# Edge stages in 26 groups of pairs (23 of four, then three, two, one) in place of 25 (24 of four, one of two)

## What is computed

```
h = relu(layernorm(x)); x = x + relu(segment_sum(att * (cat(h[src], h[dst], e) @ Wm.T + bm), dst))   # layer 0, att: softmax over dst
h = relu(layernorm(x)); x = x + rst(h)       # layer 1: (segment_sum((h @ fc.T + b) * out_deg**-.5 [src], dst)) * in_deg**-.5 + h
h = relu(layernorm(x)); x = x + gcn2(h) + h  # layer 2: two GCN convolutions with self loops, relu between
h = relu(layernorm(x)); x = x + relu(gcn2(h) + h)  # layer 3: the same with other weights
```

## Time and profile before

| | us |
|---|---|
| time, median of 3 runs (2416.01, 2422.07, 2416.51) | 2416.51 |
| the profiled execution | 2418.93 |
| its span in the profile | 2417.1 |
| PE busy | 1823.6 (75%) |
| DVE busy | 1857.2 (77%) |
| ACT busy | 1381.3 (57%) |
| POOL busy | 1778.8 (74%) |

### The profile page before, as it was taken

One profiled execution on the slowest core, in us unless ns is written; L12 is line 12 of the kernel. 1 busy time (PEld: TensorE's weight loads), 2 busy tenths in 40 slices (PEclk: granted clock), 3 DMA queues, 4 the chain that ended last, 5 costly groups with the idle time before them and its releaser, 6 DMA issues.

```text
span 2417.1 us, 26454 instructions
## 1 busy us (share of the span) xinstructions
PE 1823.6 (75%) x6414; PEld 890.1 (37%) x6414; DVE 1857.2 (77%) x3047; ACT 1381.3 (57%) x3108; POOL 1778.8 (74%) x1776
## 2 busy tenths in 40 slices
PE   3888888874998378778999767768999788879700
PEld 1433443322444134334444333334444344434300
DVE  7999976646888577887999678877999699978500
ACT  2766776532887144436888534436888555548500
POOL 7777777776777777747777677747777577777777
PEclk9999999986999699889999888879999799989955
DMA  3344322225777345434444356554444354542200
GB/s 72 91 123 129 107 72 72 72 77 133 225 244 225 94 157 160 130 108 114 126 124 130 104 168 179 167 165 109 131 130 127 110 139 135 139 118 82 70 21 22
DMA packets 220666, 295.96 MB, mean 122 GB/s; under 512 B 78636, under 2 KB 84905, under 8 KB 220388
## 3 DMA queue, kind: packets, MB, share of 16 engines
q1 hardware_dynamic: 164068, 243.35, 30.9%
q0 software_dynamic: 56448, 50.92, 11.6%
HBM read 152.99 MB, written 141.77 MB: 122 GB/s over the span
## 4 chain that ended last, share of the span: by engine, by line
POOL 34%; issue 16%; DVE 15%; PE 5%; ACT 5%; DMA 1%; DVEq 0%; POOLq 0%; SPq 0%; ACTq 0%
POOL mn_ring L540 25%; POOL out_dram L1921 8%; PE bank L1210 4%; DVE node_h L1420 3%; DVE mn_total L1599 3%; DVE node_x L1444 1%; DVE mn_scaled L1615 1%; DVE node_h L1465 1%; ACT node_square L1339 1%; DVE mn_ring L1584 1%; DVE node_mean L1427 1%; ACT node_std L1323 1%; DMA mn_ring<-slot_rows,addr_i 1%; PE bank L1204 1%; DVE node_res L1438 1%
## 5 line engine op out<-in xcount | busy, mean ns | idle before, releaser
L540 POOL DMA_INDIRECT mn_ring<-slot_rows,addr_i x980 | 971.2, 991 | 375.3 <-issue 296.8
L1210 PE MATMUL bank<-node_x,center 128*128 128x512 f32 x492 | 254.4, 632 | 75.4 <-DVE node_h L1420 71.1
L1219 PE MATMUL bank<-node_h,wconv 128*128 128x512 f32 x492 | 272.1, 637 | 0.0
L1214 PE MATMUL bank<-node_square,mean 128*128 128x512 f32 x492 | 268.7, 629 | 3.7 <-ACT node_std L1318 2.8
L1339 ACT ACTIVATE node_square<-bank 128x512 f32<-128x512 f32 x246 | 145.6, 592 | 209.7 <-PE bank L1210 209.6
L540 POOL DMA_INDIRECT found<-node_table,look_i x196 | 209.4, 1068 | 72.5 <-issue 63.9
L1921 POOL DMA_INDIRECT out_dram<-keep,scat_i x196 | 200.0, 1020 | 62.4 <-issue 62.1
L540 POOL DMA_INDIRECT xin<-in_x_dram,src_i x192 | 194.9, 1015 | 63.1 <-issue 57.6
L1224 PE MATMUL bank<-node_act,wconv 128*128 128x512 f32 x442 | 239.0, 624 | 2.7 <-ACT node_act L1333 2.7
L540 POOL DMA_INDIRECT xin<-in_x_dram,dst_i x192 | 193.0, 1005 | 58.5 <-issue 58.5
L1333 ACT ACTIVATE node_act<-bank,bias 128x512 f32<-128x512 f32 x246 | 170.5, 693 | 93.1 <-PE bank L1219 92.9
(11 more groups left out here) (345 smaller groups left out, 3896.2 us busy)
## 6 DMA issues: line engine op xcount, KB each, us to landing
out_dram<-node_rows SPq DMA_DIRECT2D x98, 256.0 KB, 3.3
mn_rin<-res SPq DMA_DIRECT2D x96, 256.0 KB, 3.8
slot_rows<-node_rows SPq DMA_DIRECT2D x96, 256.0 KB, 2.1
slot_rows<-keep SPq DMA_DIRECT2D x96, 256.0 KB, 2.0
mn_fcol<-f_rows SPq DMA_DIRECT2D x192, 128.0 KB
node_x_in<-in_x_dram SPq DMA_DIRECT2D x76, 256.0 KB
res<-mn_x SPq DMA_DIRECT2D x72, 256.0 KB, 2.9
mn_ring<-slot_rows,addr_i POOLq DMA_INDIRECT x980
```

The lines of the kernel that those rows point to most:

```text
L540: return eng.indirect_dma_start(out=dest, out_offset=None, in_=table, in_offset=bass.IndirectOffsetOnAxis(ap=index, axis=0))
L1210: pe.matmul(bank[i][:, :], C["center"][:, :], src, start=True, stop=True).then_inc(s["centered"][i], 1)
L1214: pe.matmul(bank[4][:, :], C["mean"][:, :], nd.square[:, i - 1, :], start=True, stop=True) \
L1219: pe.matmul(bank[5 if i == 2 else 1][:, :], C["wconv"][:, 2 * i - 4, :], nd.h[i][:, u % 2, :], start=True, stop=True) \
```

## The change

A table `PAIRS` gives the number of pairs of each group: 23 groups of four, then three, two and one; `STEPS` = 26. `before(g)` is the number of pairs in front of group g. All of `main_phase` reads its sizes and offsets from these; so do `node_ticks`, `ORDER` and the last entry of `CLEAR`. The front phase and `LOCALS` stay with GROUPS = 25. With the new count of steps `node_ticks` gives the totals 23, 36, 61, 75, 100 after A to E and 117 before the last step of F, which takes 13. Steps 0 to 22 have a tick in A, C and E; in B the odd steps up to 21, in D the even steps up to 22; in F the last one before the lump is step 21 in place of 20. `AHEAD` grows from 22 to 24 units.

```diff
+PAIRS = [GP] * (HQ // GP - 1) + [3, 2, 1]
+STEPS = len(PAIRS)
...
-CLEAR = (16, 19, 21, 23, GROUPS - 1)
+CLEAR = (16, 19, 21, 23, STEPS - 1)
...
-        if g == GROUPS - 1:
+        if g == STEPS - 1:
             due += GAP[st]
-        elif g < GROUPS - QUIET[st]:
+        elif g < STEPS - QUIET[st]:
             due += SHARE[st]
-        upto = TICKS if (st, g) == ("F", GROUPS - 1) else min(int(due), TICKS)
+        upto = TICKS if (st, g) == ("F", STEPS - 1) else min(int(due), TICKS)
...
-ORDER = [(st, g) for st in STAGES for g in range(GROUPS)]
+ORDER = [(st, g) for st in STAGES for g in range(STEPS)]
...
+def before(g):
+
+    return sum(PAIRS[:g])
...
         def w_of(g):
-            return pairs_of(g) * P
+            return PAIRS[g] * P
...
         def of_group(a, g):
-            return a[:, g * W:g * W + w_of(g)]
+            return a[:, before(g) * P:before(g) * P + w_of(g)]
...
-        n = GROUPS
+        n = STEPS
...
-                                         0.0 if g == 0 else total[:, 1 - i % 2, W - 1:W], ALU.mult, ALU.add) \
+                                         0.0 if g == 0 else total[:, 1 - i % 2, w_of(g - 1) - 1:w_of(g - 1)], ALU.mult, ALU.add) \
...
                     for j in range(tiles(g)):
-                        t = 2 * GP * g + j
+                        t = 2 * before(g) + j
...
-                        q = upto * GP + pairs_of(upto) - 1
+                        q = before(upto + 1) - 1
```

More of the change, by code:

```diff
@@ L1505, in w_of @@
         def w_of(g):
-            return pairs_of(g) * P
+            return PAIRS[g] * P
         def tiles(g):
-            return 2 * pairs_of(g)
+            return 2 * PAIRS[g]
         def rows3(a, g):
@@ L1523, in scale @@
         def scale(col, g):
-            return wide(col, g, 2 * GP * g)
+            return wide(col, g, 2 * before(g))
         def flat(a):
             return a.rearrange("p (t f) -> (p t) f", f=F)
-        n = GROUPS
+        n = STEPS
         order, ticks = ORDER, TICKS_OF
@@ L1902, in fetch @@
                         gp.wait_ge(s["h_kept"][1], 16 * h_uses(n, 1))
-                    elif st == "B" and 2 * GP * (g + 1) > TILES - LOOK_LAST >= 2 * GP * g:
+                    elif st == "B" and 2 * before(g + 1) > TILES - LOOK_LAST >= 2 * before(g):
                         gp.wait_ge(s["late"], mark["all"])
@@ L1955, in turn_rows @@
                         pe.wait_ge(s["mixed"], i - n)
-                    for j in range(pairs_of(g)):
+                    for j in range(PAIRS[g]):
                         c = slice(j * P, j * P + P)
```

## The result

The changed kernel takes 2430.24 us (median of 6 runs, 2427.46 to 2434.50), against 2416.52 for the kernel before in the same comparison. The ratio is 1.0052, with a 95% interval of 1.0041 to 1.0064: 12.6 us slower, between 9.9 and 15.5 (the medians lie 13.7 apart). The forecast was 2433, or +16.4, and slower.

A forecast was written before the change was run, and what follows sets the result against it. The prediction took six runs of POOL plus four handovers, where compute drains, to bound the kernel. Its terms, 6.1 + 5.3 + 2.7 + 3.0 + 0.9 - 2.2 + 0.6 = +16.4 on the median 2416.51, gave 2433 us, range 2421 to 2442.

The forecast's parts named there:

- C to D: Handover from stage C to D: a tick in step 22, then smaller steps, 22.7 us for 16.6; +6.1 us (4.5 to 7.5).
- E to F: Handover from stage E to F: same shape as C to D, 24.3 us for 19.0; +5.3 us (4 to 7.5).
- B to C: Handover from stage B to C: four small finishes in place of three, 33.1 us for 30.44; +2.7 us (1.5 to 4.5).
- D to E: Handover from stage D to E: ticks move to even steps, scan 22 comes 3.4 us earlier; +3.0 us (0.5 to 7).
- sends: POOL's sends after F's gathers: five ticks leave this stretch at 0.55 us each; -2.2 us (-5 to 0).
- front and A: A to B handover +0.9 us (0 to 3.5); front phase, two more units, +0.6 us (0 to 1.5).
- the cover of 4.5 us: Before B's first gather: addresses ready 4.5 us ahead of it; they come 5.0 later, 0.5 over the cover.
- Only the last group counts: Rival: drains begin when the last gathers land, so a last group of one pair shortens them; -11 us, 2405; chance 0.07.
- The tick is mostly absorbed: Rival: slack behind POOL hides the tick in step 22; C and E pay 2 us each, D nothing; +5, 2421; chance 0.13.
- Small groups take as long as large ones: Rival: engine rounds, not columns, set small steps; B, D 7 us each, A 3.5, C, E 7.5 each; +31, 2447; chance 0.12.

The follow-up runs named there:

- groups alone: The new groups (23 of four pairs, then 3, 2, 1) with the ticks where the kernel before had them: 2423.38 us, ratio 1.0023 to the kernel before.
- ticks alone: The kernel before with its 25 groups, plus a tick in step 22 of C and E: 2424.65 us, ratio 1.0031.
- one tick fewer: The kernel before with its 25 groups, without the tick in step 21 of B to E: 2410.18 us; with the new groups 2408.65 us.

## Why the prediction was right, and where it was off

The direction and the size held: 2433 against 2430.24, inside 2421 to 2442. By steps, profile of after against profile of before, with the share of groups (groups alone less before) and ticks (after less groups alone):

| step | forecast | measured | groups | ticks |
|---|---|---|---|---|
| C to D | +6.1 | +7.3 | +3.3 | +4.0 |
| E to F | +5.3 | +3.9 | -0.1 | +4.0 |
| B to C | +2.7 | +1.2 | +1.2 | 0.0 |
| D to E | +3.0 | +1.7 | +1.9 | -0.2 |
| sends | -2.2 | -3.8 | +0.7 | -4.5 |
| front and A | +1.5 | -0.6 | | |

Each of these is also shifted by how long before the last gather scan 22 came, and E's most: it came 2.14 us before the end of that gather in the profile of before, 3.39 with the groups alone and 4.06 after the change. Read from scan 22 to F's gather, E took 18.97, 20.08 and 24.75 us, so +5.8 for the change (groups +1.1, ticks +4.7), close to the +5.3 of the forecast; C took 16.63, 19.37 and 23.95, so +7.3 (groups +2.7, ticks +4.6). Scan 22 of E after the change:

```profile
1887.16 1.27 DVE L1606 TENSOR_TENSOR_SCAN mn_total<-same,mn_total,bank 128x512 f32<-128x512 uint8 x1
```

- *That the drains bound it.* Right. The handovers carry 14.1 us, more than all of the difference in spans, and two experiments that touch only ticks or only groups move them and the time together.
- *C and E: a tick step of 10.2, steps of 3.9 and 3.2, an end of 5.4.* The first and last are right (10.14 and 5.44). The small steps in C were mis-sized: 4.74 and 3.63. The forecast took off time for the columns, from steps of before at the higher level. Here the clock has fallen, so that the product of three pairs takes longer (1.62) than that of four did (1.13) in C of before; in E of before that of four took 1.70. Timeline of the product, in C of the changed kernel, then in C and in E of the one before; then windows of the drains (A:B us, PE, PEld, DVE, ACT, POOL busy, PEclk, DMA share, GB/s), C of before, E of before, C of after:

```profile
1345.65 1.62 PE L1980 MATMUL bank<-mn_scaled,wconv 128*128 128x384 f32 x2 [2.46 <-DVE mn_scaled L1622]
```

```profile
1335.62 1.13 PE L1973 MATMUL bank<-mn_scaled,wconv 128*128 128x512 f32 x2 [2.80 <-DVE mn_scaled L1615]
...
1883.87 1.70 PE L1973 MATMUL bank<-mn_scaled,wconv 128*128 128x512 f32 x2 [2.81 <-DVE mn_scaled L1615]
```

```profile
1334.00:1344.00 10.00, 4.83 (x18) 2.59 (x18) 5.37 (x8) 3.84 (x14) 2.37 (x3) 0.88 0.24 76
1882.00:1893.00 11.00, 6.15 (x14) 2.83 (x15) 4.68 (x6) 3.97 (x15) 1.65 (x2) 0.60 0.22 69
```

```profile
1344.00:1357.00 13.00, 7.85 (x18) 3.92 (x19) 5.69 (x13) 5.19 (x20) 0.00 (x0) 0.57 0.23 74
```

  In C of before the granted clock was 0.88 of the higher level over the drain, in E only 0.60. That is why step 22, with the same work, took 4.71 us there and 5.75 here: 0.57 of the 1.04 are the product's, and 0.45 the transposes before the next scan. It also accounts for the groups' 2.7 from scan 22 on in C and only 1.1 in E: with the groups alone both drains run almost wholly at the lower level and take about as long (19.37 and 20.08), while before E's was the slower one (16.63 and 18.97). The forecast had both step lengths from the rows and named the clock in the lower bound of C, but its sum for C goes on from steps at the higher level, and so stands too low. In E its 4.7 and 3.8 came out as 4.76 and 3.62, and the end of 5.6 as 6.18.
- *B: +2.7.* The steps were 7.95, 7.70, 6.25, 10.20, together 32.1 against the forecast's 7.8, 8.1, 6.7 and 10.5, 33.1. The mechanism held (an additional group costs its fixed parts), steps 23 and 24 were sized 0.4 and 0.5 too long and the end 0.3. The operation sizes were right: one pair 0.28 to 0.29 where 0.285 was forecast, so the fixed 0.15 of an operation stands. The 60 ns of the Trainium skill, Perfetto Trace Analysis, section Optimizing Scalar/DVE Operations, are called an engine-busy time there, of which a profiled latency is about twice as much. The prediction's estimate leaves that out: by 120 ns, again an estimate, ten operations would cost 0.3 us less, not 0.9.
- *D: +3.0, by a tick that moves to an even step.* Right in its mechanism: scan 22 came 8.28 us before the end of the last gather where it was 4.06, 4.2 earlier (3.4 forecast); the tick step took 11.35 (11.3), then 6.97, 5.67 and 9.47 (7.0, 5.8, 9.8). The scan 0.8 earlier than forecast and the last parts 0.5 shorter make +1.7 of the +3.0. The additional tick costs D nothing (-0.2 in the table): before it, step 21 has none, and scan 22 comes earlier against the gathers. The sum's waits in D, answering to the earlier trace rows:

```profile
  DMA mn_ring<-slot_rows,addr_i: 27.4, 13
```

- *A: the cover of 4.5 us is used up.* Right: B's first gather now waits for `addr_i`, by 0.17 us more than the usual 0.30. But it comes at 804.89, not at 806 to 808, since A itself was earlier than before (its scan 22 at 773.15, not 774.89). The rest of front and A can't be told: POOL starts B between 800.2 and 805.5 us in the nine profiles.
- *Sends: -2.2 at 0.55 a tick.* Mis-sized: 262.1, 261.3 and 258.2 us with 18, 16 and 13 ticks (before, ticks alone, after). The slow sends belong to those ticks that normalise their unit and not to all: in each of the nine profiles the last send of over 1.1 us starts 0.4 us after the last `node_x_in<-node_x_in,node_h` of DVE, which is the end of such a normalising, though node work goes on for another 32 to 34 us. Before, 11 of the 18 did, now 6 of 13, so all five that left are of the slow kind: 3.8 us, 0.77 each. That price is this change's only: over the kernels that were run the sends take 258.2, 261.3, 262.1, 263.1, 265.2 and 266.0 us with 6, 9, 11, 13, 15 and 19 such ticks, which is 0.2 to 1.1 for one more and 0.6 on average. The nine profiles together bear out what the prediction read from one send: 123 sends that start beside `node_res<-node_x,node_h`, a DVE sum of two SBUF tensors, take 1.38 us on average, 102 beside `node_x_in<-node_x_in,node_h` 1.17, but 141 beside a DVE operation that reads one of its two tensors from PSUM (`node_h<-bank,node_std`) 0.98, as 1037 beside no DVE operation do. That speaks against what the Trainium skill, SBUF — State Buffer, section Who interferes with whom, infers of a tensor_tensor and descriptor generation. By that inference the prediction's sum would be higher by the term itself, 2.2, and not by the 2.7 that it gives.
- *The rivals.* Only the last group counts: false for the change, where the sums of the groups 23 to 25 wait for no gather in B to E. With one tick fewer the handovers do get 1.7 us shorter with the new groups, far from its 11; but the last group's sum waits for no gather there either, so that its condition was never met and stays untested. The tick is mostly absorbed: false in C and E (4.0 each, where it put 2), true in D; its terms sum to +6.0, not to the +5 given. Small groups take as long as large ones: false in B and D (+1.2 and +1.7, not 7), partly so in C, where three pairs took as long as four.

What the forecast missed as a whole is how near the ticks themselves stood to an optimum: it saw that the drain of C followed the last gather by 6 us and took that as given. Taking one tick out of the end of the four stages gains 8.5 us with the old groups, and with the new ones brings the time from 5.6 above to 10.9 below the kernel before.

Left open: what set the moment at which the granted clock fell (in the kernel before between 1341 and 1342 us in C, 8 us after scan 22, but between 1884 and 1885 in E, 3 us after it, with the same work before both); why E's compute runs about 2 us later against its gathers in one profile than in others, and whether 3, 2, 1 is better or only no worse than one group of two once the ticks end early.

## What to carry to other kernels

Where one engine feeds stages in runs, and a barrier lies between them, cost a change at the drains: list the last steps with their lengths, and look which of them wait for data and which only for their own chain. Smaller last pieces are cheap when the pieces before them have caught up with the feeding engine: here they then cost nothing that could be measured, and a gain was not shown. Where compute is behind, the additional piece costs its fixed part, 1.1 to 2.7 us for a drain here (groups alone less before, from scan 22 on). A count of pieces that also places other work (here `GROUPS` in the planner of ticks) moves that work with it, and that was about half of the loss (7.5 us for the ticks alone, 5.6 for the groups alone).

## What the runs showed of the hardware

The clock that TensorE is granted fell within each of these drains. In the first ten or eleven microseconds after the last tick's step it was 0.88 of the higher level in one drain and 0.60 in another of the same kernel (C and E of before), and a step with no change in work lasted 4.7 us in the one and 5.7 in the other. A product of 384 columns at the lower level (1.2 GHz) took 1.62 us, one of 512 at the higher (2.4 GHz) 1.13. So a step with less work for TensorE took as long as a fuller one: 4.74 us with three pairs, 4.71 with four, in C.

An indirect send of GpSimd takes longer beside a DVE operation with two inputs in SBUF: 1.38 us on average (0.98 to 1.50) beside `node_res<-node_x,node_h`, against 0.98 beside no DVE operation.
